# A layernorm, state-space and mixture-of-experts kernel: the skip term `D * xn` moves from the end of the program into the running sum of each chunk

## The reference, cut to what matters

```python
xn = _layernorm(x)                       # x: 2 x 2048 x 512, so S = 4096 rows of D = 512
# state-space branch: N = 16 states per channel, scan over time
h = a_t * h + b_t                        # a = exp(delta * A), b = delta * B * silu(conv(xn))
s = einsum('btdn,btn->btd', h_all, C_in) + xn * D_param      # the skip term is the last product
# mixture of experts: 8 experts, top 2, capacity 1024 rows each, hidden 2048
y = sum over the two experts of gate * (gelu(xn @ fc1 + b1) @ fc2 + b2)
out = x + s * silu(y)
```

## Time and profile before

| what | value |
|---|---|
| three runs | 2046.97, 2015.56, 2047.07 us (median 2046.97) |
| the profiled execution's own time | 2014.59 us |
| its span, first to last instruction | 2012.7 us |
| busy over the span | PE 92%, DVE 92%, POOL 65%, ACT 61% |
| front stage / main loop / end | 0 to 254 / 254 to 1936 / 1936 to 2012.7 us |
| granted PE clock | full from 259 us to the end of the main loop |

### The profile page before, as it was taken

The page is one execution under the profiler, slowest core; times in us unless marked ns, Lnnn a source line. Parts: engine busy times, 40 slices in busy tenths (PEclk is TensorE's granted clock), DMA queues, the critical chain, the costliest instruction groups (busy, mean ns, idle before and its releaser), DMA issues. The chain is left out here.

```text
span 2012.7 us, 29247 instructions
## 1 busy us (share of the span) xinstructions
PE 1847.6 (92%) x8968; PEld 1449.4 (72%) x8968; DVE 1853.9 (92%) x2004; ACT 1222.6 (61%) x1772; POOL 1303.5 (65%) x621
## 2 busy tenths in 40 slices
PE   6998189999999999999999999999999999999940
PEld 3332078888888878887888788888888888888830
DVE  7998579899998999899989998999899989999899
ACT  3577585556755665566556655666565755675543
POOL 1388466578667776677567866786678667866530
PEclk9999699999999999999999999999999999999975
DMA  9168643346212531244124511351145113621396
GB/s 315 68 97 114 172 173 116 115 162 153 74 64 103 138 86 61 73 146 109 63 73 142 120 68 64 124 121 63 63 150 127 63 63 111 177 74 63 108 355 242
DMA packets 83894, 240.06 MB, mean 119 GB/s; under 512 B 11713, under 2 KB 12609, under 8 KB 71505
## 3 DMA queue, kind: packets, MB, share of 16 engines
q1 hardware_dynamic: 67120, 205.07, 31.1%
q0 software_dynamic: 16416, 33.70, 9.2%
q10 hardware_dynamic: 256, 0.26, 0.1%
HBM read 170.45 MB, written 68.55 MB: 119 GB/s over the span
## 5 line engine op out<-in xcount | busy, mean ns | idle before, releaser
L1188 DVE TENSOR_TENSOR_SCAN a_sb<-a_sb,state,ub_sb 128x512 f32<-128x512 f32 x512 | 894.2, 1785 | 9.9 <-issue 6.0
L1097 POOL TENSOR_TENSOR ub_sb<-u_sb,brow_sb 128x1024 f32<-128x1024 f32 x256 | 629.5, 2459 | 401.7 <-DVE a_sb L1188 398.9
L829 PE MATMUL pm<-xTh,w1l 128*128 128x512 f32 x1024 | 423.0, 413 | 6.8 <-POOL w1l L1082 5.7
L829 PE MATMUL pm<-w2h,hl 128*128 128x512 f32 x1024 | 422.8, 413 | 0.2 <-DVE hl L1168 0.2
L831 PE MATMUL pm<-w2h,hh 128*128 128x512 f32 x1024 | 401.8, 392 | 0.0
L831 PE MATMUL pm<-xTh,w1h 128*128 128x512 f32 x1024 | 401.6, 392 | 0.0
L830 PE MATMUL pm<-w2l,hh 128*128 128x512 f32 x1024 | 398.6, 389 | 0.0
L830 PE MATMUL pm<-xTl,w1h 128*128 128x512 f32 x1024 | 398.1, 389 | 0.0
L1159 DVE SCALAR_TENSOR_TENSOR s_acc_keep<-pt,ct_keep,s_acc_keep 128x512 f32<-128x512 f32 x480 | 352.0, 734 | 19.7 <-PE pt L861 19.0
L976 ACT ACTIVATE a_sb<-delta_sb,neg_a_keep 128x512 f32<-128x512 f32 x512 | 330.2, 713 | 6.7
L861 PE MATMUL pt<-ident_keep,a_sb 128*128 128x128 f32 x2048 | 306.3, 272 | 5.7 <-DVE a_sb L1188 5.7
(11 more groups left out here) (163 smaller groups left out, 1950.8 us busy)
## 6 DMA issues: line engine op xcount, KB each, us to landing
raw_keep<-in_w SPq DMA_DIRECT2D x64, 1024.0 KB, 4.8
brow_sb<-b_chunks SPq DMA_DIRECT2D x128, 256.0 KB
moe_rows<-zeros SPq DMA_DIRECT2D x8, 1280.0 KB, 6.4
xn_rows<-xn_sb SPq DMA_DIRECT2D x8, 1024.0 KB, 9.1
delta_chunks<-ln_sb SPq DMA_DIRECT2D x8, 1024.0 KB
u_chunks<-xn_sb SPq DMA_DIRECT2D x16, 512.0 KB
delta_sb<-delta_chunks SPq DMA_DIRECT2D x8, 1024.0 KB, 8.1
u_sb<-u_chunks SPq DMA_DIRECT2D x16, 512.0 KB, 3.9
```

The lines of the kernel that those rows point to most:

```text
L829: pe.matmul(out, sl, mh, start=start, stop=False)
L1097: pool.tensor_tensor(ub[:, h], u[:, 2 * h:2 * h + 2, :], brow[:, m % 2:m % 2 + 1, :].to_broadcast([P, 2, CH]), ALU.mult).then_inc(s_["bmul ...
L1188: op = dve.tensor_tensor_scan(abuf[:, m, 2 * h + k, :], abuf[:, m, 2 * h + k, :], ub[:, h, k, :], state[:, ds(col, 1)], ALU.mult, ALU.add)
```

## The change

For each chunk, SP loads the four 128 x 512 blocks of `xn_rows` into the places as soon as each place's old content has been stored (`load_skip`). DVE multiplies the block by D in place (`skip`, one 128 x 512 instruction a place, in steps 3 to 6 of the first quarter), and the sum over the states is added to that, so that its first instruction in each place is line 1159's form instead of line 1157's. SP works in pairs: it stores places 0 and 1, loads them, stores 2 and 3, loads the row of B for m = 2, loads 2 and 3, loads the row of B for m = 3. At the end of the program `normalise`, `scale` and `add_skip` are gone (32 ACT and 32 DVE instructions, and the small `shift`), parts 12 to 15 of `y` get rooms of their own (`late[:, 11]` and `ub`), and SP issues all 16 loads of `y` ahead of the first store.

```diff
+                def load_skip(tb):
+                    if begins(e):
+                        sp.wait_ge(s_["x_turned"], TPC + tb + 5)
+                    else:
+                        sp.wait_ge(s_[f"s_out{tb}"], 16 * e)
+                    sp.dma_start(s_acc[:, tb, :], dr.xn[ds(e * CH + tb * P, P)]).then_inc(s_[f"skip_in{tb}"], 16)
...
-                    if first and not begins(e):
-                        for tb in range(TPC):
-                            store_s(tb)
+                    if first:
+                        for pair in ((0, 1), (2, 3)):
+                            if not begins(e):
+                                for tb in pair:
+                                    store_s(tb)
+                            if pair[0] == 0:
+                                for tb in pair:
+                                    load_skip(tb)
                     for m in range(2, NPQ):
                         load_b(it, q, m)
+                        if first and m == 2:
+                            for tb in (2, 3):
+                                load_skip(tb)
...
-            for p in range(NP - 4):
+            for p in range(NP):
                 load_y(p)
-            for p in range(2):
-                store(p)
-            for p in range(NP - 2, NP):
-                load_y(p)
...
+            for p in range(NP):
                 store(p)
...
-            for p in range(NP):
-                normalise(p)
             for p in range(NP):
                 silu(p)
...
                 if starts:
-                    dve.wait_ge(s_[f"s_out{tb}"], 16 * e + 16)
-                    dve.tensor_scalar(acc, h, c, None, ALU.mult).then_inc(s_["summed"], 1)
-                else:
-                    dve.scalar_tensor_tensor(out=acc, in0=h, scalar=c, in1=acc, op0=ALU.mult, op1=ALU.add).then_inc(s_["summed"], 1)
+                    dve.wait_ge(s_["skipped"], TPC * e + tb + 1)
+                dve.scalar_tensor_tensor(out=acc, in0=h, scalar=c, in1=acc, op0=ALU.mult, op1=ALU.add).then_inc(s_["summed"], 1)
+
+            def skip(e, tb):
+                dve.wait_ge(s_[f"skip_in{tb}"], 16 * e + 16)
+                dve.tensor_tensor(s_acc[:, tb, :], s_acc[:, tb, :], d_row[:], ALU.mult).then_inc(s_["skipped"], 1)
...
+                        if first and LAG <= s + 1 < LAG + TPC:
+                            skip(e, s + 1 - LAG)
...
-            scale(0)
-            for p in range(NP):
-                if p + 1 < NP:
-                    scale(p + 1)
-                add_skip(p)
             gate(0)
```

More of the change, by code:

```diff
@@ L646, in main_loop @@
         warm = sb("warm", [P, 2])
-        d_row, shift, zeros = sb("d_row", [P, D]), sb("shift", [P, NT]), sb("zeros", [P, D])
+        d_row, zeros = sb("d_row", [P, D]), sb("zeros", [P, D])
         pm = psum("pm", [P, 4, 512])
@@ L652, in main_loop @@
             b2_in staged add_staged added0 added1 cleared biased carried act_at dve_at pool_at sp_at
-            d_row zeroed shift xn skip whole silu gated sum out
+            d_row zeroed skip_in0 skip_in1 skip_in2 skip_in3 skipped silu gated sum out
             """ + " ".join(f"x_chunk{c} s_chunk{c} y_part{2 * c} y_part{2 * c + 1}" for c in range(NCH)))
@@ L659, in main_loop @@
         y_rows = ([abuf[:, m] for m in range(NPQ)] + [part[:, 0:TPC, :], part[:, TPC:, :]] +
[L660 to L665, removed]
+                  [late[:, 11], ub[:].rearrange("p h k d -> p (h k) d")])
         LAST = NQ * NCH
@@ L784, in _ @@
             for tb in range(TPC):
-                sp.wait_ge(s_[f"s_out{tb}"], 16 * NCH)
+                sp.wait_ge(s_[f"s_out{tb}"], 16 * (NCH - 1))
             sp.wait_ge(s_["exp"], 8 * LAST + 1)
@@ L1016, in _ @@
             chunks(act, chunk)
[L1018 to L1026, removed]
             def silu(p):
@@ L1030, in silu @@
                 act.activation(half(y_rows, p), half(y_rows, p), ACT.Silu).then_inc(s_["silu"], 1)
-            act.wait_ge(s_["shift"], 1)
-            act.wait_ge(s_["l2"], 8 * LAST + 1)
-            act.wait_ge(s_["scan"], 8 * LAST + 2)
-            for p in range(NP):
-                normalise(p)
             for p in range(NP):
@@ L1126, in _ @@
             dve.wait_ge(s_["cleared"], 3)
-            for name, credits in (("x_lo", 2), ("acc_free", 8), ("scan", 2), ("summed", 4), ("biased", 1),
-                                  ("s_out0", 16), ("s_out1", 16), ("s_out2", 16), ("s_out3", 16)):
+            for name, credits in (("x_lo", 2), ("acc_free", 8), ("scan", 2), ("summed", 4), ("biased", 1)):
                 dve.sem_inc(s_[name], credits)
-            mean, rstd = (keep[k][:].rearrange("p c j -> p (c j)") for k in ("mean", "rstd"))
-            dve.scalar_tensor_tensor(out=shift[:], in0=mean, scalar=-1.0, in1=rstd, op0=ALU.mult, op1=ALU.mult).then_inc(s_["shift"], 1)
             def low_x(e, t, bank):
@@ L1154, in sum_up @@
                 if starts:
-                    dve.wait_ge(s_[f"s_out{tb}"], 16 * e + 16)
-                    dve.tensor_scalar(acc, h, c, None, ALU.mult).then_inc(s_["summed"], 1)
-                else:
-                    dve.scalar_tensor_tensor(out=acc, in0=h, scalar=c, in1=acc, op0=ALU.mult, op1=ALU.add).then_inc(s_["summed"], 1)
+                    dve.wait_ge(s_["skipped"], TPC * e + tb + 1)
[3 more added lines that the diff above has]
+                dve.tensor_tensor(s_acc[:, tb, :], s_acc[:, tb, :], d_row[:], ALU.mult).then_inc(s_["skipped"], 1)
             for t in range(TILES):
                 low_x(0, t, pm[:, t, :] if t < TPC else pt[:, t - TPC, :])
+            dve.wait_ge(s_["d_row"], 16)
             def chunk(e):
@@ L1209, in _, with gate @@
                 sum_up(NCH, 0, s, True, False)
[L1211 to L1217, removed]
+            def gate(p):
                 if p < NP - 2:
                     dve.wait_ge(s_[f"s_chunk{p // 2}"], 16)
[L1220 to L1224, removed]
                 dve.wait_ge(s_["silu"], p + 1)
@@ L1230, in add_x @@
                 dve.tensor_tensor(half(x_rows, p), half(x_rows, p), half(s_rows, p), ALU.add).then_inc(s_["sum"], 1)
-            dve.wait_ge(s_["d_row"], 16)
             dve.wait_ge(s_["summed"], GROUPS * NCH + 4)
-            scale(0)
-            for p in range(NP):
-                if p + 1 < NP:
-                    scale(p + 1)
-                add_skip(p)
             gate(0)
```

## The result

| | before | changed |
|---|---|---|
| median of seven runs | 2015.06 us | **2034.56 us** |
| lowest and highest | 2010.38, 2047.07 | 2027.62, 2039.34 |
| ratio, with its 95% interval | | **1.0099** (1.0082 to 1.0115) |
| the profiled execution's own time | 2014.59 | 2036.06 |
| its span | 2012.7 | 2034.3 |

The changed kernel is slower by 1.0%, some 20 us. The forecast time was 2035.0. Here and in the table of experiments a median counts every run, and a ratio leaves out the few runs over 1.5% above the fastest of their kernel (of before, two here at 2047 and one beside e5 to e7; three of e5's fourteen; one of e7's four).

What follows compares the result with a forecast made beforehand. PE was taken to set the main loop's pace and DVE to bound the end. From 2014.6 us, 38 added by `skip` taking turns with POOL, less 17.5 at the end, gave 2035 us; range 2014 to 2069.

Steps and rivals of the forecast that it cites:

- Step 1: Chunk 2's first quarter: `skip` 0 waits for POOL to 701.7, so the scans end at 705.3 instead of 704.1, +1.2 us.
- Step 2: Chunk 2's first quarter: `skip` 1 waits 1.7 us for POOL; the fourth scans end at 713.2 instead of 709.0, +4.2 us.
- Step 4: Chunk 2's first quarter: `skip` 3 waits for POOL's moved product; the scans end at 720.4 instead of 715.8, +4.6 us.
- Step 5: Rest of the first quarter: 0.2 us lost in order, PE starts the next quarter 4.8 us later; 8 chunks give 38 us.
- Step 3: PE in the first quarter: the scan delay is all on its path, and its wait for `low_h` 4 lies within it.
- Zero: SP's refills and later row of B in the first quarters: they land in time and cost nothing.
- the refills come late: Rival in the loop: store and refill take over 13 us, `skip` waits for data, 2 us a chunk more, 2051; 5%.
- The end: After the main loop: 36.35 us of DVE work go, half hidden behind scatter-adds and first load; gain 17 to 18 us.
- The clock rival: PE in each first quarter: pauses bring 7 us at half clock, costing 3.5 a chunk, 28 in all, 2063; 8%.
- the forecast proper: Whole kernel: 38 us lost in the loop, bounds 30 to 48, own range 2024 to 2046; 70%.
- the transfers at the end: Rival at the program's end: transfers bound it, so the gain would be 10 us, 2043; end gains nothing or all, 5%.
- the one case that ends faster: Rival in the loop: `skip` does not take turns with POOL, costing 4 us instead of 38, 2001; 12%.

Runs made afterwards that it cites:

- e5: Changed kernel with products 0 and 2 issued before, 1 and 3 behind, the second and third scan pairs of each first quarter; 2004.84 us, ratio 0.9956 to before.
- e7: Changed kernel with the end's loads and stores of `y` put back into the order of the kernel before; 2032.97 us, ratio 1.0101 to before.
- e2: Changed kernel with the product reading one operand from PSUM instead of the row of D (31 of 32), D left out; 1999.54 us, ratio 0.9927 to before.
- e3: Changed kernel without the products with D, refills and waits kept; 1999.47 us, ratio 0.9922 to before.
- e4: Changed kernel with SP's order unpaired: four stores, row of B for m = 2, four refills, row for m = 3; 2049.71 us, ratio 1.0179 to before.
- e1: Changed kernel with the products in adjoining pairs right behind the scans of steps 4 and 6; 2030.77 us, ratio 1.008 to before.
- e6: Changed kernel with a scatter-add issued between POOL's fourth product and the low half of the second weight tile; 2044.6 us, ratio 1.0171 to before.

## Why the prediction was right in its sum and wrong in its chances

**The steps in the loop, by chunk 2** (11.50 us taken off the times after). Step 1: the scans behind the first product end at 716.84, that is 705.34; forecast 705.3, +1.2. Step 2: the fourth scans end at 724.67, that is 713.2; forecast 713.2, +4.2, with 1.75 us waited by product 1 (1.7). Step 4: the next scans end at 731.90, that is 720.4; forecast 720.4, +4.6. Step 5: the quarter is 4.4 us longer here, 4.7 in the mean of seven chunks, 5.4 in chunk 0; forecast 4.8. The later quarters gave nothing back. Sum 38.0; forecast 38. e2 and e3 show that it was the turns, as taken. That chunk 0 came out near the others is luck: it was not worked out, and its product of place 0 lasts 2.23 us and not 5.6.

**Step 3 was right in the sum and not in its detail.** I expected PE's wait for the fourth scans to grow and a wait of 2 to 3 us for `low_h` beside it. The second came (2.60), the first did not in chunk 2, for a reason in the clock rival below.

**SP.** The first refill was issued at 691.9 (forecast 692), the second pair's at 701.2 (700.8), the row of B for m = 3 at 703.4 (701.2, 2 us off and without effect). Landing 2.5 to 7.9 us, median 2.7: the least is below my lower bound of 2.9, the rest inside my bounds, though the transfers were not "half empty" (a DMA share of 0.74 from 688 to 705 us before). "Zero" was right, with room: store and first refill take 5.9 us together (700.17 to 706.04), and not 13. The rival "the refills come late" (over 13 us together, 2 us a chunk more, 2051) was priced right: e4 makes it 15.2 us together, its first quarter of chunk 2 is 2.1 us longer (59.61 against 57.54), and it takes 2049.7.

**The end.** Gain 18.0; forecast 17 to 18. DVE idle 18.18 before the first gate; forecast 17 to 19.

**The clock rival came true by half.** The granted clock did leave its full level in the loop, in the first quarters of chunks 0, 1, 2, 4, 5 and 7. The prediction names this as a sign of its being wrong; the sign came, and the time did not follow it. The stretch at the same place of chunk 2 and of chunk 3; columns: us, busy of PE, PEld, DVE, ACT, POOL, PEclk, DMA share, GB/s:

```profile
721.80:725.20 3.40, 3.40 (x11) 2.29 (x10) 3.40 (x4) 0.00 (x0) 1.81 (x2) 0.53 1.05 195
935.80:939.20 3.40, 2.19 (x12) 1.52 (x11) 3.40 (x4) 0.00 (x0) 1.81 (x2) 1.00 1.06 176
```

And PE in chunk 3, where the clock stayed full:

```profile
934.69 0.47 PE L833 MATMUL pm<-w2h,hl 128*128 128x512 f32 x1 [2.58 <-DVE hl L1156]
...
938.90 0.65 PE L865 MATMUL pt<-ident_keep,a_sb 128*128 128x128 f32 x4 [1.21 <-DVE a_sb L1176]
```

At full clock PE is done with its products early and stands 1.21 us for the scans. At half (1.2 GHz) it does the same products in just that time. Both chunks' first quarters last 57.54 us. In e7, with the same loop, the clock fell in chunks 2, 3, 5 and 6 instead, and its first quarters of chunks 2 to 7 last 57.4 to 57.7 us with the fall or without. I had priced 3.5 us a chunk (7 us at half clock, all of it on the path); it was some 3.4 us, under a wait that was there anyway, and cost nothing. In the loop of before, and in e2, e3 and e5, where PE never pauses for over 1.5 us, the clock stayed full. In chunk 2 the fall follows PE's pauses of 0.57 and 2.60 us. So here it goes with the pauses that the turns make and is no cost beside them.

**The step that failed** is the one from the time to the chances: "A measurement of this kernel tells about 2% from no change, 40 us. The forecast is +1.0%, so it is within". The prediction gives no source for the 2%, and no row shows it; the three runs shown spread by 1.6% (2015.6 to 2047.1), but the profiled execution (2014.6) and one of them agreed to 1 us. The comparison of the seven runs of the changed kernel with five of before has an interval of 0.17% to either side, less than a tenth of what I assumed, and from 1.0082 to 1.0115 it does not hold 1. My own cases said slower almost throughout: the forecast proper at +20 us, and the clock, the late refills and the transfers at the end above it, 88% together, against 12% for the one case that ends faster. The forecast should have been given out as "slower by a measurable 1%", not as "the same". The upper part of the range (2051 to 2069) was there for the level of the two runs at 2047, for the clock and for late refills, and wasn't needed.

In the experiments two of my expectations were wrong, for reasons that carry more than the prediction did: e1 (DVE's adjoining products do not hold the port, in 13 of 16 pairs) and e4 (a refill behind four stores is there after 5.3 us and not 2.9). The time of e6 also lay above its range.

## What to carry to other kernels

Count an added DVE instruction with two SBUF operands not at its own 0.6 us but by whether POOL is inside a product when it asks; here it made 38 us of what costs 3 us at most when POOL has no part in it (e2), and putting each one where DVE would wait anyway or where POOL's next product has not begun took 30 of them back (e5). Work that leaves the end of a program gives only what was not covered by the last transfers (18 of 36 us), while work that enters a loop pays in each pass. And before a forecast is called "no change", ask what interval the runs will have: an effect of 1% with a known sign is a result.

## What the hardware showed that I had not expected

- POOL's two adjoining products kept DVE out over both: the product of place 0 asked at 708.36, the second of them began at 710.42, and DVE got in at its end, 713.39. DVE's adjoining products did not keep POOL out in 13 of 16 pairs (e1: 3.44 us for two, POOL's multiply at 714.01 between them) and did in three (1.26 us for two at 1365.09), and a pair of scans did not either (e6: 5.63 us, POOL's low half at 707.89 between them). By the section of the Trainium skill named at e2 (SBUF — State Buffer) whoever issues first has the port for the whole instruction; the products of places 1 and 3 agree (they ask 0.48 us after POOL and last 2.4 us), but here an instruction of POOL that began 2 us after DVE had asked still went first.
- The granted clock fell to its half level for some 3.4 us around or after two pauses of PE, of 0.44 to 0.87 and 2.56 to 2.64 us, in the first quarters of five of chunks 1 to 7 (0.53 and 1.00 in the stretches above). Chunks 2 and 3 have pauses that agree to 0.02 us, and the clock fell in one only; in e7 it fell in four of the eight chunks, and not in the same ones. What decides between them stays open.
- Nine executions took from 273.0 to 287.7 us to their first transpose, though the work up to there is nearly the same. That is more than e7 or e6 moved, and a reason to compare the loop and the end by themselves.
